# Two-layer convolution attention on one core: the broadcast of the maxima placed behind the second scores, one larger VectorE share of the subtraction, an embedding added without a table, and x loaded in halves

## The reference, cut to what matters

```python
# layer 0
xn = group_norm(x, gn_w, gn_b)                       # 32 groups
q, k, v = split(einsum('oc,bchw->bohw', qkv_w, xn) + qkv_b)
w = softmax(einsum('ncq,nck->nqk', q, k * scale))    # per head, 2304 x 2304
h = proj_w @ (w applied to v) + proj_b + x
# layer 1
q = concat(h, emb) @ Wq;  k = concat(h, emb) @ Wk;  v = h @ Wv
# emb: 32 channels depend on the image row alone, 32 on the image column alone
o = softmax(q k^T * scale) v
out = o @ Wout + bout + h
```

## Time and profile before

| | |
|---|---|
| median of 3 runs | 4218.99 us (4218.84 to 4219.61) |
| profiled execution | 4219.53 us, span 4217.8 us |
| TensorE (PE) busy | 4099.4 us, 97% |
| VectorE (DVE) busy | 3278.0 us, 78% |
| ScalarE (ACT) busy | 2763.7 us, 66% |
| GpSimd (POOL) busy | 1773.6 us, 42% |

### The profile page before, as it was taken

The page is one execution under the profiler, slowest core; times in us unless marked ns, Lnnn a source line. Parts: engine busy times, 40 slices in busy tenths (PEclk is TensorE's granted clock), DMA queues, the critical chain, the costliest instruction groups (busy, mean ns, idle before and its releaser), DMA issues. The chain is left out here.

```text
span 4217.8 us, 88347 instructions
## 1 busy us (share of the span) xinstructions
PE 4099.4 (97%) x30024; PEld 1901.6 (45%) x30024; DVE 3278.0 (78%) x4032; ACT 2763.7 (66%) x3557; POOL 1773.6 (42%) x572
## 2 busy tenths in 40 slices
PE   7999999999999999998999989999999999999989
PEld 4554344444444444444555544444444444444445
DVE  3111999999999999997322239999999999999962
ACT  1112888888888888886000018888888888888840
POOL 0000455555555555553100005555555555555520
PEclk9999999999999999999999999999999999999999
DMA  4112000101000000011333220101000000000116
GB/s 176 75 75 94 10 27 19 37 13 32 20 28 22 22 23 26 26 49 51 118 102 127 97 95 9 31 20 32 19 28 24 22 22 26 24 21 30 42 47 215
DMA packets 157932, 208.41 MB, mean 49 GB/s; under 512 B 9008, under 2 KB 144304, under 8 KB 156848
## 3 DMA queue, kind: packets, MB, share of 16 engines
q1 hardware_dynamic: 137712, 179.28, 12.9%
q10 hardware_dynamic: 20160, 28.32, 1.8%
HBM read 113.19 MB, written 94.37 MB: 49 GB/s over the span
## 5 line engine op out<-in xcount | busy, mean ns | idle before, releaser
L589 POOL TENSOR_TENSOR prob<-prob,mx 128x1056 f32<-128x1056 f32 x564 | 1752.6, 3107 | 2237.0 <-DVE prob L589 2237.0
L753 ACT ACTIVATE prob<-psum_att 128x768 f32<-128x768 f32 x1728 | 1353.9, 822 | 938.6 <-PE psum_att L684 535.4
L684 PE MATMUL psum_att<-qst,kst 64*128 64x384 f32 x6912 | 1286.2, 504 | 30.3 <-DMA kst<-qk_scratch 17.8
L769 ACT ACTIVATE prob<-prob 128x1152 f32<-128x1152 f32 x1152 | 1292.9, 1175 | 16.5 <-POOL prob L589 14.5
L695 PE MATMUL psum_att<-prob,vst 128*32 128x384 f32 x13824 | 1239.3, 490 | 0.4 <-issue 0.4
L856 DVE TENSOR_TENSOR run<-psum_att,run 128x768 f32<-128x768 f32 x1152 | 1057.8, 947 | 24.3 <-PE psum_att L684 23.1
L589 DVE TENSOR_TENSOR prob<-prob,mx 128x1248 f32<-128x1248 f32 (+1 forms) x576 | 972.1, 1688 | 0.0
L684 PEld LDWEIGHTS psum_att<-qst,kst 64*128 64x128 f32 x6912 | 621.9, 187 | 575.2 <-issue 174.2
L695 PEld LDWEIGHTS psum_att<-prob,vst 128*32 128x32 f32 x13824 | 393.7, 109 | 718.4 <-issue 529.1
L870 DVE TENSOR_TENSOR two_tiles<-prob 128x768 f32<-128x768 f32 x564 | 534.4, 948 | 0.0
L309 PE MATMUL psum<-xc_l,wq 128*128 128x384 f32 x1536 | 504.0, 489 | 9.9 <-DVE qk_l L406 4.8
(11 more groups left out here) (56 smaller groups left out, 1690.9 us busy)
## 6 DMA issues: line engine op xcount, KB each, us to landing
qk_scratch<-qk_l SPq DMA_DIRECT2D x48, 768.0 KB, 3.5
v_scratch<-vo_l SPq DMA_DIRECT2D x24, 768.0 KB, 3.5
qst<-qk_scratch SPq DMA_DIRECT2D x96, 192.0 KB, 2.4
kst<-qk_scratch SPq DMA_DIRECT2D x96, 192.0 KB, 2.4
vst<-v_scratch SPq DMA_DIRECT2D x96, 192.0 KB, 2.5
att_scratch<-ob ACTq DMA_DIRECT2D x96, 192.0 KB, 1.9
attc_l<-att_scratch SPq DMA_DIRECT2D x24, 768.0 KB, 5.4
x_sb<-in_x SPq DMA_DIRECT2D x8, 1152.0 KB, 14.0
```

Source lines behind the costliest of these rows:

```text
L589: return engine.tensor_tensor(x, x, m, ALU.subtract)
L684: mm = nc.tensor.matmul(psum[:, 2 * k + e, 0:CH], kst[rows, (3 * c + k) * P:(3 * c + k + 1) * P], qst[par][rows, :], start=True, stop=True ...
L753: nc.scalar.activation(prob[par][:, :, s, :], s_banks(k)[:, :, 0:CH], ACT.Copy).then_inc(copied, 1)
L769: nc.scalar.activation(x, x, ACT.Exp, scale=SCALE).then_inc(exp_done, 1)
```

## The change

It has five edits. (1) `broadcast_max` stands behind the scores of c = 1 instead of ahead of them; its signal is given for each of the three query parts, so `copy_max` waits for its own part, and VectorE's maxima of slots 3 to 5 wait for the part of their bank. (2) Before each of its three transposes `spread_den` waits for the copy of that part's bank, instead of for all three beforehand. (3) VectorE subtracts 304 columns instead of 208 in group 3, GpSimd 80 instead of 176. (4) In the middle stage there are no tables. Each eviction adds the row values (384 positions are 8 image rows) and a second VectorE addition in SBUF adds the column values, one tile behind. TensorE's banks wait for the first addition alone (`qk_read`), stores for the second. The output projection of chunk 0 comes ahead of the embedding products, and GpSimd has no work there. (5) Each x tile is loaded by two DMAs of half the positions with a counter each, and `bn_stats` of part 0 and part 3 wait for them.

```diff
-SHIFT_DVE = 208
+XH = 2
+SHIFT_DVE = [208, 208, 208, 304, 208, 208]
@@ norm_part
-    if j == 0:
-        dve.wait_ge(gn["x_in"][n], 16)
+    if j % (JB // XH) == 0:
+        dve.wait_ge(gn["x_in"][n][j * XH // JB], 16)
@@ load_x
-                sp.dma_start(gn["x"][:, c, b * HW:(b + 1) * HW],
-                             x_d[c * P:(c + 1) * P, b * HW:(b + 1) * HW]).then_inc(gn["x_in"][n], 16)
+                for h in range(XH):
+                    tokens = slice(b * HW + h * HW // XH, b * HW + (h + 1) * HW // XH)
+                    sp.dma_start(gn["x"][:, c, tokens], x_d[c * P:(c + 1) * P, tokens]).then_inc(gn["x_in"][n][h], 16)
@@ middle stage, TensorE
+            if out_proj:
+                pe.wait_ge(w_in[out_proj["w_at"]], 16)
+                out_tiles(0, 0)
             if emb:
...
-            if out_proj:
-                pe.wait_ge(w_in[out_proj["w_at"]], 16)
-                out_tiles(0, 0)
...
-                            pe.wait_ge(qk_out, MT * i + m - 3)
+                            pe.wait_ge(qk_read, MT * i + m - 3)
@@ middle stage, VectorE
+            def add_cols(i, m):
+                half, mt = divmod(m, CT)
+                dve.wait_ge(qk_read, MT * i + m + 1)
+                nc.vector.tensor_tensor(image(qk[half][:, mt, :]), image(qk[half][:, mt, :]), emb_cols(m), ALU.add)\
+                    .then_inc(qk_out, 1)
...
-                            nc.vector.tensor_tensor(qk[half][:, mt, :], qk_bank(m), emb_of(i, m), ALU.add)\
-                                .then_inc(qk_out, 1)
+                            nc.vector.tensor_tensor(image(qk[half][:, mt, :]), image(qk_bank(m)), emb_rows(i, m),
+                                                    ALU.add).then_inc(qk_read, 1)
+                            if m > 0:
+                                add_cols(i, m - 1)
+                            if m == MT - 1:
+                                add_cols(i, m)
@@ attention, TensorE: broadcast_max, spread_den, body
-                mm.then_inc(broadcast, 1)
+                    mm.then_inc(broadcast, 1)
...
                 for r in range(3):
+                    bank_free(t + 3, DEN_SPREAD_AT, r)
                     mm = nc.tensor.transpose(psum[:, 2 * r, CH:512], dwide[:, r, :], ident)
...
-                    if c == BROADCAST_AT and not before(t, 1) and live(t - 1):
-                        broadcast_max(t - 1, c)
...
                     if c == DEN_SPREAD_AT and not before(t, 3) and live(t - 3):
-                        bank_free(t, c, 2)
                         spread_den(t - 3)
                     if live(t):
                         for k in range(3):
...
+                    if c == BROADCAST_AT and not before(t, 1) and live(t - 1):
+                        broadcast_max(t - 1, c)
@@ attention, ScalarE: copy_max
-                if r == 0:
-                    act.wait_ge(broadcast, t + 1)
+                act.wait_ge(broadcast, 3 * t + r + 1)
@@ attention, VectorE: maximum
                 dve.wait_ge(scored, scored_count(slot(t, s)))
+                if s // 3 == BROADCAST_AT and not before(t, 1):
+                    dve.wait_ge(broadcast, 3 * (t - 1) + s % 3 + 1)
                 if s < 6:
                     dve.wait_ge(copied, slot(t, s - 3))
```

More of the change, by code:

```diff
@@ L53, in norm_buffers @@
         gn[name + "_sem"] = ctx.enter_context(nc.semaphore(name))
-    gn["x_in"] = [ctx.enter_context(nc.semaphore(f"x_in{n}")) for n in range(N)]
+    gn["x_in"] = [[ctx.enter_context(nc.semaphore(f"x_in{n}_{h}")) for h in range(XH)] for n in range(N)]
     return gn
@@ L196, in qkv_stage @@
         qk_out = sem("qk_out")
+        qk_read = sem("qk_read") if emb else qk_out
         v_done = sem("v_done")
@@ L223, in pairs_of_chunks, with image, emb_rows, emb_cols @@
             pair(NCH // 2 - 1, True)
[L225 to L229, removed]
+        def image(x):
+            return x.rearrange("p (h w) -> p h w", w=SIDE)
+        def emb_rows(i, m):
+            return bufs["emb_parts"][:, m, bass.ds(i % JB * (CH // SIDE), CH // SIDE)].unsqueeze(2)\
+                .broadcast_to([P, CH // SIDE, SIDE])
+        def emb_cols(m):
+            return bufs["emb_parts"][:, m, SIDE:2 * SIDE].unsqueeze(1).broadcast_to([P, CH // SIDE, SIDE])
         @block.sync
@@ L356, in _ @@
                 pairs_of_chunks(act, pair)
[L358 to L363, removed]
         @block.vector
@@ L384, in input_chunk @@
                     d.then_inc(xc_ready, 1)
+            def add_cols(i, m):
[3 more added lines that the diff above has]
+                    .then_inc(qk_out, 1)
+            input_chunk(0, 0)
             if emb:
                 dve.wait_ge(emb_copied, 1)
[L388 to L393, removed]
             def pair(it, last):
@@ L400, in pair @@
                         if emb:
-                            if is_block(i, 0):
-                                dve.wait_ge((emb_dve, emb_pool)[m % 2], m // 2 + 1)
-                            elif mt == 0:
+                            if mt == 0 and not is_block(i, 0):
                                 dve.wait_ge((q_stored, k_stored)[half], 16 * i)
                             dve.wait_ge(qk_mm, MT * i + m + 1)
-                            nc.vector.tensor_tensor(qk[half][:, mt, :], qk_bank(m), emb_of(i, m), ALU.add)\
-                                .then_inc(qk_out, 1)
+                            nc.vector.tensor_tensor(image(qk[half][:, mt, :]), image(qk_bank(m)), emb_rows(i, m),
[4 more added lines that the diff above has]
+                                add_cols(i, m)
                         if norm and is_block(i, 1):
@@ L755, in copy_max @@
             def copy_max(t, par, r):
-                if r == 0:
-                    act.wait_ge(broadcast, t + 1)
-                    if not before(t, 2):
-                        act.wait_ge(dve_shifted, group(t - 2, KC - 1))
-                        act.wait_ge(pool_shifted, group(t - 2, KC - 1))
+                act.wait_ge(broadcast, 3 * t + r + 1)
+                if r == 0 and not before(t, 2):
+                    act.wait_ge(dve_shifted, group(t - 2, KC - 1))
+                    act.wait_ge(pool_shifted, group(t - 2, KC - 1))
                 nc.scalar.activation(mx[par][:, :, r * P:(r + 1) * P], s_banks(r)[:, :, CH:512], ACT.Copy)\
@@ L829, in body @@
                     pool.wait_ge(dve_shifted, group(t, c))
[L830 removed]
+                    shift_part(nc.gpsimd, par, c, SHIFT_DVE[c], CH).then_inc(pool_shifted, 1)
             with pool.Fori(0, NB // 2 - 1) as it:
@@ L841, in reduce @@
                 if not before(t, 1):
-                    dve.wait_ge(broadcast, t)
+                    dve.wait_ge(broadcast, 3 * t)
                 nc.vector.tensor_reduce(mcol[:, :, r], s_banks(r)[:, :, CH:512], AX.X, ALU.max).then_inc(reduced, 1)
@@ L876, in shift @@
                 dve.wait_ge(copied, slot(t, 3 * c + 2))
-                shift_part(nc.vector, par, c, 0, CH if last(t) else SHIFT_DVE).then_inc(dve_shifted, 1)
+                shift_part(nc.vector, par, c, 0, CH if last(t) else SHIFT_DVE[c]).then_inc(dve_shifted, 1)
             def sum_den(t, k):
```

6 lines of the change are left out of this document (1 added, 5 removed).

## The result

The changed kernel takes 4231.31 us (median of 12 runs, 4228.62 to 4232.47), the kernel before 4219.52 in the same comparison (12 runs, 4218.53 to 4221.30). The ratio is 1.0026, with an interval of 1.0019 to 1.0034: slower by a quarter of a per cent, 11.8 us. The profiled execution took 4231.29 us, its span is 4229.5.

A forecast was written before the change was run, and what follows sets the result against it. TensorE's order was taken to meet the VectorE and ScalarE chain at `turn_den`. 4219.53 + 16 (attention) - 8 (middle stage) - 1.4 (x halves) = 4226.1 us; 8-in-10 range 4198 to 4242, likeliest case 4216 to 4236.

The forecast's parts named there:

- chain of 8.43: VectorE and ScalarE work from the first maximum of c = 1 to `turn_den`, 8.43 us with no slack.
- Broadcast to maximum: At c = 1, slot 3's maximum starts 0.65 us after the broadcast's transposes start; bounds 0.45 and 0.75.
- Rival A: Broadcast's wait hidden, slot 3's maximum released by 8.16; only the spread's 0.15 won: 4197 us; chance 0.22 including cases towards the forecast.
- B: Attention block: the whole 0.58 us of waits is won if the 8.43 run has unseen slack: 4159 us; chance 0.05.
- Waits of the copies at c = 1: TensorE's scores of c = 1 wait for ScalarE's later copies of c = 0: 0.04 us charged, bounds 0 and 0.2.
- rival C: VectorE's larger share delays copies of c = 0, so TensorE waits at c = 1: 4240 us at 0.2, 4276 unhidden; chance 0.22.
- Spread: Denominators' spread behind the scores of c = 3: its 0.15 us wait for the third bank's copy goes wholly.
- Period: One attention loop block takes 32.44 us against 32.26, +0.18; +16 us over 88 blocks.
- Middle stage: Without tables, chunk 0's q and k tiles lose VectorE's wait and the slow clock: together -8 us, bounds -4.3 and -8.4.
- Rival D: In the middle stage TensorE waited for the weights, not the tables: -1.4 alone, 4234 us; chance 0.05.
- x in halves: Norm stage: three `bn_stats` parts remain after the last landing, statistics end near 16.8: -1.4 us, bounds 0 and -2.1.
- GpSimd's part by elements: GpSimd's group 3 subtraction scales with elements, 3.10 x 480/1056 = 1.41 us, ending before VectorE's next subtraction starts.

The follow-up runs named there:

- split kernel: Changed kernel with the broadcast's first part ahead of the scores of c = 1 and the other two behind them: 4180.01 us, ratio 0.9904.

## Why the prediction came out as it did

The median is 5.3 above the 4226.0, within the likeliest case's own range. It lies on the side of slower, beyond the 4227.4 that separates it from no change. The prediction gave slower and no change the same chance, 0.36, so the side was not forecast. The mechanism was right: the broadcast holds back the maximum of slot 3, the chain of 8.43 carries this to `turn_den`, and attention loses more than the middle stage wins. Its sizes, step by step:

- **Broadcast to maximum, 0.65.** Measured 0.65 (7.91 to 8.56), and 0.65 in the changed kernel without edit 3. Rival A, in which this wait is hidden, fell with it: the maximum would have had to start by 8.16. B fell too, as the chain has no slack.
- **The chain of 8.43.** Measured 8.41 (1633.00 to 1641.41).
- **Waits of the copies at c = 1, 0.04.** This is the step that failed in size: it is 0.11. I had counted the second and third copy as spaced like TensorE's slots, which they are (0.70), but each slot's weight load now begins only at its copy's end, and I gave that no price. So the broadcast came at 7.91 instead of 7.84, the maximum of slot 3 at 8.56 instead of 8.49, and `turn_den` at 16.97 instead of 16.92. That is rival C in a small form. Without edit 3 the period is 0.10 shorter.
- **Spread, -0.15.** Right; edit 2 alone measured -13.5, 88 times 0.153.
- **Period, 32.44.** Measured 32.48: +19.2 instead of +16, 3 of the 5.3 missed. The edges add 1 and the other stages 1.
- **Edges of the layers, 0 with bounds of 2.** Measured +1.1 ahead of layer 0's first turn, -1.8 in its first blocks and its end, +1.7 in layer 1: +1 in all. That the sum is small is in part luck, as they cancel.
- **Middle stage, -8.** Measured -8.1 (-7.4 in the q and k tiles of chunk 0, -0.7 at the start). Rival D (weights) fell with it: the earlier trace rows had named the right releaser. Of the 7.4, 4.76 was idle time. The granted clock was 0.69 of full speed over the old stall, so in part at the lower level (1.2 GHz), and it is 1.00 in its place now. The Trainium skill, TensorE: Matmul & The Clock Gate, section What's actually happening, has the clock of an idle engine halved, which would account for the rest; the trace agrees with it.
- **x in halves, -1.4.** The norm stage won 1.2 between these two traces, and some 0.7 on average over the twelve, since the last half lands at 15.50 and the rest took 1.5. Alone the edit measures nothing, and by the first turn of layer 0 nothing is left of the gain: that the first product follows was right, that the gain stays to the end I had taken for granted.
- **Signs.** The broadcast stands 2.25 behind its scores (2.14) and has no gap. Idle time ahead of slot 3's maximum 0.98 (0.8 to 1), ahead of `turn_den` 0.52 (0.7, less by the later slots), none at the spread, subtraction 1.47 (1.45), statistics done at 17.04 (16.8).
- **GpSimd's part by elements, 1.41.** It took 1.86, and this step failed: the 3.10 of the earlier trace rows was scaled as a whole, though it holds a wait. GpSimd and VectorE's `pair_tiles`, before and after, and GpSimd's first part of layer 0 before:

```profile
1716.68 0.95 DVE L870 TENSOR_TENSOR two_tiles<-prob 128x768 f32<-128x768 f32 x1
1627.82 0.95 DVE L870 TENSOR_TENSOR two_tiles<-prob 128x768 f32<-128x768 f32 x1
1627.98 1.86 POOL L588 TENSOR_TENSOR prob<-prob,mx 128x480 f32<-128x480 f32 x1 [4.29 <-DVE prob L588]
442.57 2.44 POOL L589 TENSOR_TENSOR prob<-prob,mx 128x1056 f32<-128x1056 f32 x1 [442.12 <-DVE prob L589]
```

In both blocks GpSimd starts while VectorE adds two tiles in SBUF, and they overlap for 0.8. At 442.57 no such addition runs beside it, and the same 1056 elements take 2.44 instead of 3.10. So about 0.7 is the wait for VectorE, and the rest is 2.3 ns an element: 0.7 + 1.1 = 1.8 for 480 elements. It didn't matter for the time: GpSimd ends at 1629.84, VectorE's subtraction starts at 1629.68 and takes 1.47. The Trainium skill, SBUF — State Buffer, section Who interferes with whom, has an instruction of VectorE with two inputs in SBUF and one of GpSimd that reads SBUF contend for a shared port. The trace agrees, and in this direction too, which the prediction left out: there VectorE's subtraction waits for GpSimd, here GpSimd waits for VectorE's addition.

I priced edit 3 only as a part of the whole. Priced alone in the kernel before, by the earlier trace rows, it is +0.6 a block, and that would have shown how near to the edge the copies of c = 0 lie.

## What to carry to other kernels

- Where two engines are both nearly always busy, follow one round trip (here matmul, maximum, copy, bank) and look for the point where the chain and the engine's own order meet within a tenth of a microsecond. A step moved off one of them is worth nothing if it is late for the other.
- A group of small steps that release different consumers need not move together. One part in front and two behind won 51 us over all three behind.
- Edits on one chain don't add. Time them in the order in which they would be kept; the same larger share cost 53 us, cost 8 and won 12, by what stood next to it.
- Before a duration is scaled by its elements, look for a wait inside it: the same instruction took 3.10 beside another engine's addition and 2.44 without it.

## What the runs showed of the hardware

- GpSimd's subtraction of 128 x 1056 elements takes 3.11 us where VectorE adds two SBUF tiles beside it for 0.8, and 2.44 where it doesn't; that of 128 x 480, always beside such an addition, takes 1.86 (spans of GpSimd are rough). The 3.11 and 1.86 alone would read as 0.8 us fixed, which they are not.
- A group of transposes inside running matmuls takes less than in proportion: two 0.35, three 0.48, six 0.80 from their start to the next matmul of another kind.
- VectorE's next step starts 0.65 behind the start of a group of transposes of which it needs the first two, in three kernels (changed, edit 1 alone, changed without edit 3), whether it had been idle for 0.98 or 0.21. In the split kernel it is 0.63.
- 576 KB halves of x land about 1.4 us apart (the last six at 8.38, 9.79, 11.22, 12.63, 14.07, 15.50). The last comes later than the last whole tile does: 15.50 to 15.87 in the eight traces with halves, 14.83 to 15.35 in the four with whole tiles.
